# Products of the last-but-one stage placed among units 2 to 27 of the last stage, instead of among units 2 to 37

## The chip, the core and the metric

The kernel runs on one core of a Trainium2 chip. The metric is the device time of one execution in microseconds, the median of a few runs. Times of single instructions come from one profiled execution, counted from its first instruction.

## What is computed

```python
# x (1024, 24, 1024) f32, W1 (1024, 24), b1 (1024,), W2 (1024, 1024), b2 (1024,)
h = sigmoid(einsum('bts,st->bs', x, W1) + b1)
y = h @ W2.T + b2
```

The input x is about 100 MB, so nearly all of the traffic is the reading of x. The sum over t is elementwise work on x with a weight for each (s, t); the product h @ W2.T is a matrix product of 1024 x 1024 x 1024.

## The kernel before

**Tiling.** The work is cut into five stages (`STAGES`, line 19). A stage is a block of 512 rows of the batch (j, four tiles of 128) and two to four chunks of 128 columns s. The first two stages do the first 512 rows; stages 2, 3 and 4 do the other 512 rows with 3, 3 and 2 chunks. Stage 4 is the last.

**Units.** Within a stage the 24 values of t are split. The first few (six in the last stage) go to GpSimd: it multiplies their tiles by the weights and adds them up in the batch-major layout (tile `nat`, lines 485 and 495). The rest go through the PE array: a *unit* is one t and one chunk. TensorE turns its four 128x128 tiles by transposes into one PSUM bank (line 232, `xbank`), and VectorE multiplies the bank by the weight and adds it to `acc` (line 354). One more unit for each chunk turns GpSimd's sum (line 352 on VectorE). The last stage has 38 units: 0 to 31 are sixteen values of t with two chunks each, 32 and 33 turn GpSimd's sum, and 34 to 37 are the last two values of t. A unit may be turned once the bank that it takes is free, that is once the unit six before it has been added (line 221).

**Loads.** SP issues all loads of x in one order. A ring load (tile `ring`, five slots, line 201) brings one t for all chunks of the stage, so in the last stage 512 KB for two units. It waits until the last unit that read its slot, five loads before, is turned (line 200): the load of units 36 and 37 waits for unit 25. A `nat` load (line 195, 256 KB in the last stage) stands ahead of some ring loads in the queue and waits for GpSimd's sums.

**Products.** When a stage's `acc` is complete, ScalarE takes the sigmoid to `h` (line 431), and `h` and W2 are each split into a high and a low part. Each of eight outputs (128 rows x 512 columns, in one of two banks `pbank`) is summed from three products for each chunk: `h_hi` with `w_hi`, `h_hi` with `w_lo`, `h_lo` with `w_hi` (line 301, 128x512). They are issued during the *next* stage, between its units, in an order written out by `steps_due(i, v)`: after unit v of stage i, the products of stage i - 1 are issued up to step `steps_due(i, v)`. For the last stage there are 8 x 9 = 72 products; `REST` = 12 of them come behind the last unit (lines 318 to 320). VectorE adds an output to `y` (line 371) after a unit that `outs_due`, the same count divided by nine, names; so its additions of outputs stand in a fixed place between additions of units. Outputs 0 and 1 are summed with their low products behind both outputs' high ones, so output 0 is complete with product 15. An output from the third on waits on TensorE for the addition of the one two before, which had its bank (line 284).

**The end.** ScalarE's sigmoids of the last stage wait at line 450 until all eight outputs of the stage before are summed, and at line 452 for the units' additions, chunk by chunk. The last stage's own products come behind (line 332, 48 of them), then the additions and the stores.

The functions that set the order and those that follow it are these.

Of the kernel before, what the change touches and what calls it, by code (L numbers as in the profile page):

```python
# [27 lines left out]
def rec_kernel(nc, x, W1, b1, W2, b2, out):  # L28
# [12 lines left out]
    REST = 12  # L41
# [9 lines left out]
    units = []  # L51
# [38 lines left out]
    with ExitStack() as ctx:  # L90
# [64 lines left out]
        def steps_of(i):  # L155

            return 3 * chunks[i] + (fate[i] == "keep")


        def steps_due(i, v):  # L160

            steps = OUTS * steps_of(i - 1)
            if i == LAST:
                lead = chunks[i]
                return max(0, -(-(v - lead + 1) * (steps - REST) // (len(units[i]) - lead)))
            lead = 2 * chunks[i]
            span = len(units[i]) * 4 // 5 - lead
            return max(0, min(steps, -(-(v - lead + 1) * steps // span)))

        def outs_due(i, v):  # L170

            return steps_due(i, v) // steps_of(i - 1)
# [43 lines left out]
        def _(pe):  # L216
# [90 lines left out]
            for i in range(NS):  # L307
                for v in range(len(units[i])):
                    turn_unit(i, v)
                    if i == 0 and v in SETS:  # L310
                        turn_set(SETS[v])
                    if i == 0 and v in W2S:
                        turn_w2(W2S[v])
                    if i > 0:
                        for k in range(steps_due(i, v - 1) if v else 0, steps_due(i, v)):
                            product_step(i - 1, k)
# [213 lines left out]
```

## Time and profile before

| | us |
|---|---|
| median of 3 runs | 315.55 (315.52 to 315.67) |
| the profiled execution | 316.05 |
| its span, first to last instruction | 314.3 |
| TensorE busy | 262.0 (83%) |
| VectorE busy | 247.3 (79%) |
| GpSimd busy | 214.9 (68%) |
| ScalarE busy | 50.9 (16%) |
| mean granted TensorE clock | 0.973 |

The busy shares are averages over five stages and an end, which have different limits. The slices of the page show where the transfers stop, the chain of waits which engine holds the end, and timelines of one engine what stands between two instructions.

### The profile page before, as it was taken

Reading aid. Unit: us, or ns where it says so; the run is one execution under the profiler, and the core shown is the slowest. Engines: PE = TensorE matmul, PEld = TensorE weight load, DVE = VectorE, ACT = ScalarE, POOL = GpSimd, SP = SyncE. Lnnn points to the kernel's source line nnn. Section 1 sums busy time; section 2 is a strip of 40 time slices with the busy share of each in tenths; the row PEclk is TensorE's granted clock in tenths of the full one; section 3 lists DMA queues with packets and bytes.
Section 4 is the critical chain, followed back from the end, with each engine's and each line's share of the span. In section 5 each row is a group of like instructions: output and inputs, shape, how many; then the busy total and the mean of one; then the engine's idle time right before and its main releaser. Section 6 shows DMA issues by size and latency. Waiting matters only on the chain.

```text
span 314.3 us, 4779 instructions
## 1 busy us (share of the span) xinstructions
PE 262.0 (83%) x1761; PEld 223.9 (71%) x1761; DVE 247.3 (79%) x368; ACT 50.9 (16%) x85; POOL 214.9 (68%) x125
## 2 busy tenths in 40 slices
PE   0957768658889999999799999858999977989994
PEld 0946758558767888888678888746888876667773
DVE  0639998729998988889977888868887897788665
ACT  4111213202262100100600000040111113000020
POOL 3128766635469999994999977479988749994000
PEclk9989999969999999999799999979999999999999
DMA  7999999999999999999999999999999999996007
GB/s 214 392 389 387 386 387 387 401 388 386 387 387 385 386 387 387 387 385 381 373 373 373 385 384 382 376 384 373 374 373 374 368 351 339 344 348 202 2 0 268
DMA packets 67675, 109.48 MB, mean 348 GB/s; under 512 B 3642, under 2 KB 40514, under 8 KB 67652
## 3 DMA queue, kind: packets, MB, share of 16 engines
q1 hardware_dynamic: 67056, 107.06, 95.7%
q10 hardware_dynamic: 596, 2.11, 1.7%
q8 instruction: 14, 0.23, 0.3%
q14 instruction: 9, 0.07, 0.1%
HBM read 104.97 MB, written 4.19 MB: 347 GB/s over the span
## 4 chain that ended last, share of the span: by engine, by line
PE 50%; DMA 32%; DVE 5%; issue 5%; SPq 4%; ACT 2%; DVEq 0%; ACTq 0%
DMA ring<-in_r_x 32%; PE xbank L232 25%; PE pbank L301 20%; DVE acc L354 3%; PE xbank L332 3%; SPq L195 3%; SPq L201 2%; PE pbank L291 1%; ACT h L431 1%; DVE w_lo L361 1%; PE pbank L332 1%; ACT h_hi L456 1%; PE pbank L261 0%; ACT L431 0%; DVE acc L352 0%
## 5 line engine op out<-in xcount | busy, mean ns | idle before, releaser
L354 DVE SCALAR_TENSOR_TENSOR acc<-xbank,w,acc 128x512 f32<-128x512 f32 x280 | 200.4, 746 | 40.6 <-PE xbank L232 35.1
L232 PE MATMUL xbank<-ident,ring 128*128 128x128 f32 x1184 | 176.1, 284 | 44.3 <-DMA ring<-in_r_x 34.7
L232 PEld LDWEIGHTS xbank<-ident,ring 128*128 128x128 f32 x1184 | 146.5, 147 | 76.7 <-issue 30.7
L485 POOL TENSOR_TENSOR nat<-nat,w1all 128x768 f32<-128x768 f32 (+2 forms) x56 | 106.9, 1910 | 60.6 <-DMA nat<-in_r_x 47.8
L495 POOL TENSOR_TENSOR nat<-nat 128x768 f32<-128x768 f32 (+2 forms) x46 | 87.6, 1905 | 3.6
L301 PE MATMUL pbank<-w_lo,h_hi 128*128 128x512 f32 x112 | 48.8, 435 | 0.0
L301 PE MATMUL pbank<-w_hi,h_hi 128*128 128x512 f32 x112 | 48.5, 433 | 0.0
L301 PE MATMUL pbank<-w_hi,h_lo 128*128 128x512 f32 x112 | 41.0, 431 | 0.0
L431 ACT ACTIVATE h<-acc,b1col 128x512 f32<-128x512 f32 (+1 forms) x22 | 12.5, 600 | 99.7 <-DVE acc L354 64.0
L348 DVE TENSOR_SCALAR acc<-xbank,w 128x512 f32<-128x512 f32 x16 | 11.9, 748 | 13.8 <-PE xbank L232 11.6
L443 ACT COPY y<-pbank 128x512 f32<-128x512 f32 x16 | 9.4, 587 | 79.3 <-PE pbank L301 79.3
L301 PEld LDWEIGHTS pbank<-w_hi,h_hi 128*128 128x128 f32 x112 | 21.4, 191 | 0.5
L301 PEld LDWEIGHTS pbank<-w_lo,h_hi 128*128 128x128 f32 x112 | 21.4, 191 | 0.4
L500 POOL TENSOR_TENSOR h_lo<-h,h_hi 128x512 fp32r<-128x512 f32 x14 | 17.7, 1280 | 2.9 <-ACT h_hi L456 2.9
L301 PEld LDWEIGHTS pbank<-w_hi,h_lo 128*128 128x128 f32 x112 | 18.6, 191 | 0.5
L413 ACT CAST w_hi<-pbank 128x512 fp32r<-128x512 f32 x16 | 9.4, 586 | 40.6 <-PE pbank L261 40.6
L371 DVE TENSOR_TENSOR y<-pbank,y 128x512 f32<-128x512 f32 x18 | 12.2, 683 | 4.0 <-PE pbank L301 4.0
L261 PE MATMUL pbank<-ident,y 128*128 128x128 f32 x64 | 10.3, 285 | 1.4 <-DVE w_lo L361 1.4
L361 DVE TENSOR_TENSOR w_lo<-pbank,w_hi 128x512 fp32r<-128x512 f32 x16 | 10.9, 678 | 0.0
L352 DVE TENSOR_TENSOR acc<-xbank,acc 128x512 f32<-128x512 f32 x16 | 10.1, 680 | 0.1
L408 ACT COPY w1all<-pbank 128x512 f32<-128x512 f32 x12 | 7.0, 586 | 17.5 <-PE pbank L250 17.5
L261 PEld LDWEIGHTS pbank<-ident,y 128*128 128x128 f32 x64 | 7.7, 147 | 2.4 <-DVE w_lo L361 2.4
(37 smaller groups left out, 93.2 us busy)
## 6 DMA issues: line engine op xcount, KB each, us to landing
ring<-in_r_x SPq DMA_DIRECT2D x38, 1024.0 KB, 13.3
ring<-in_r_x SPq DMA_DIRECT2D x36, 768.0 KB, 11.1
nat<-in_r_x SPq DMA_DIRECT2D x20, 512.0 KB, 13.2
nat<-in_r_x SPq DMA_DIRECT2D x24, 384.0 KB, 11.5
ring<-in_r_x SPq DMA_DIRECT2D x18, 512.0 KB, 8.1
y<-in_L_rec_W SPq DMA_DIRECT2D x2, 2048.0 KB, 15.1
nat<-in_r_x SPq DMA_DIRECT2D x12, 256.0 KB, 8.7
out_y<-y ACTq DMA_DIRECT2D x4, 512.0 KB, 7.1
```

The lines of the kernel that those rows point to most:

```text
L232: mm = pe.transpose(xbank[u % XBANKS][:, j * P:(j + 1) * P], tile, ident[:, :])
L261: mm = pe.transpose(pbank[m % 2][:, j * P:(j + 1) * P], y[:, j, c * P:(c + 1) * P], ident[:, :])
L301: mm = pe.matmul(pbank[n % 2][:, :], a[:, c, rows], w[:, STAGES[i][1] + c, cols], start=r == 0, stop=r == per - 1)
L332: mm = pe.matmul(bank[:, :], a[:, c, j * P:(j + 1) * P], w[:, STAGES[LAST][1] + c, cols], start=c == 0 and k == 0, stop=c == chunks[LAST] ...
L348: nc.vector.tensor_scalar(total, bank, weight, None, ALU.mult).then_inc(unit_added, 1)
L354: nc.vector.scalar_tensor_tensor(out=total, in0=bank, scalar=weight, in1=total, op0=ALU.mult, op1=ALU.add).then_inc(unit_added, 1)
L361: nc.vector.tensor_tensor(w_lo[:, c, cols], pbank[m % 2][:, :], w_hi[:, c, cols].bitcast(F32), ALU.subtract).then_inc(w_lo_ready, 1)
L371: nc.vector.tensor_tensor(y[:, j, cols], bank[:, :], y[:, j, cols], ALU.add).then_inc(y_added, 1)
L431: nc.scalar.activation(h[:, c, rows], acc[:, c, rows], ACT.Sigmoid, bias=b1col[:, bass.ds(STAGES[i][1] + c, 1)]).then_inc(h_ready, 1)
L485: nc.gpsimd.tensor_tensor(slot, slot, row, ALU.mult).then_inc(nat_weighed, 1)
L495: nc.gpsimd.tensor_tensor(slot, slot, nat[:, (m - 2) % NATS, :, :n * P], ALU.add).then_inc(nat_added, 1)
L500: nc.gpsimd.tensor_tensor(h_lo[:, c, :], h[:, c, :], h_hi[:, c, :].bitcast(F32), ALU.subtract).then_inc(h_lo_ready, 1)
```

## The change

`steps_due` for the last stage divided the 60 products ahead of `REST` over all units behind the first two (`len(units[i]) - lead`, that is 36). It now divides them over 28 - 2 = 26 units, and a `min` keeps the count at 60 from unit 27 on.

```diff
             if i == LAST:
                 lead = chunks[i]
-                return max(0, -(-(v - lead + 1) * (steps - REST) // (len(units[i]) - lead)))
+                return max(0, min(steps - REST, -(-(v - lead + 1) * (steps - REST) // (28 - lead))))
```

The count is read in three places: TensorE's loop (line 315), VectorE's additions of outputs inside the stage (line 380) and the additions left over behind it (line 391). The order of instructions on ScalarE, GpSimd and SP does not change, nor does anything in stages 0 to 3.

TensorE, the last units of the stage. Before, units 33 to 37 (the first row is unit 33, which turns GpSimd's sum; `xbank` and `pbank` carry their numbers) and the first products behind them:

```order
L232 MATMUL xbank1<-ident,nat 128x128 x4
L301 MATMUL pbank1<-w_hi,h_lo 128x512 x2
L232 MATMUL xbank2<-ident,ring 128x128 x4
L301 MATMUL pbank0<-w_hi,h_hi 128x512
L232 MATMUL xbank3<-ident,ring 128x128 x4
L301 MATMUL pbank0<-w_lo,h_hi 128x512
L301 MATMUL pbank0<-w_hi,h_hi 128x512
L232 MATMUL xbank4<-ident,ring 128x128 x4
L301 MATMUL pbank0<-w_lo,h_hi 128x512
L301 MATMUL pbank0<-w_hi,h_hi 128x512
L232 MATMUL xbank5<-ident,ring 128x128 x4
L301 MATMUL pbank0<-w_lo,h_hi 128x512
```

Now, from unit 27 (the first row) to unit 37 and the products behind it:

```order
L232 MATMUL xbank1<-ident,ring 128x128 x4
L301 MATMUL pbank0<-w_hi,h_hi 128x512
L301 MATMUL pbank0<-w_lo,h_hi 128x512
L232 MATMUL xbank2<-ident,ring 128x128 x4
...
L232 MATMUL xbank0<-ident,nat 128x128 x4
L232 MATMUL xbank1<-ident,nat 128x128 x4
...
L232 MATMUL xbank5<-ident,ring 128x128 x4
L301 MATMUL pbank0<-w_hi,h_lo 128x512 x3
```

The products that stood between units 28 and 37 are gone from there; units 28 to 37 follow each other, and behind unit 37 come the twelve of `REST`, as before.

VectorE, the front of the last stage, now, from the additions of units 5 and 6 to that of output 1 (behind unit 10):

```order
L354 SCALAR_TENSOR_TENSOR acc<-xbank3,w1,acc 128x512
L354 SCALAR_TENSOR_TENSOR acc<-xbank4,w1,acc 128x512
L371 TENSOR_TENSOR y<-pbank0,y 128x512
L354 SCALAR_TENSOR_TENSOR acc<-xbank5,w1,acc 128x512
L354 SCALAR_TENSOR_TENSOR acc<-xbank0,w1,acc 128x512
L354 SCALAR_TENSOR_TENSOR acc<-xbank1,w1,acc 128x512
L354 SCALAR_TENSOR_TENSOR acc<-xbank2,w1,acc 128x512
L371 TENSOR_TENSOR y<-pbank1,y 128x512
```

Before, the addition of output 0 stood behind that of unit 7, one later, and that of output 1 behind unit 13. All six additions of outputs inside the stage have moved forward; the last one was ahead of the last three units and is now ahead of the last twelve.

## Rows read from the trace of the kernel before

**Rows 1.** The page: busy shares, then slices of the span.

```profile
PE 262.0 (83%) x1761; PEld 223.9 (71%) x1761; DVE 247.3 (79%) x368; ACT 50.9 (16%) x85; POOL 214.9 (68%) x125
...
DMA  7999999999999999999999999999999999996007
```

**Rows 2.** The chain that ended last, from 276.92: start us, us, what.

```profile
276.92 7.88 DMA ring<-in_r_x
284.80 0.14 issue
284.94 0.63 PE xbank L232 x4
285.56 0.47 PE pbank L301 x2
286.03 0.44 PE xbank L232 x4
...
294.38 0.44 PE xbank L232 x4
294.82 2.99 PE pbank L301 x13
297.80 0.03 ACTq L452
...
297.88 0.41 ACT h L431
```

**Rows 3.** Waits from 297 us on: us in total, times, longest.

```profile
ACT h L431 <- PE pbank L301: 35.8, 1, 35.8
```

**Rows 4.** Ring loads, line 201: the last (issued 284.2), then all from 250.

```profile
L201 SPq DMA_DIRECT2D ring<-in_r_x x1: 368/368/368, 284.2 to 284.2; - x1
...
DMA to landing us min/median/max: 6.1/6.1/6.1
...
DMA to landing us min/median/max: 6.1/8.0/9.5
```

**Rows 5.** Timeline of TensorE: units 4, 6, 12, 18, 24, 25, 26, 28, 36, 37.

```profile
262.61 0.63 PE L232 MATMUL xbank<-ident,ring 128*128 128x128 f32 x4 [0.98 <-DMA ring<-in_r_x]
...
264.82 0.63 PE L232 MATMUL xbank<-ident,ring 128*128 128x128 f32 x4 [0.45 <-DVE acc L354]
...
270.72 0.63 PE L232 MATMUL xbank<-ident,ring 128*128 128x128 f32 x4 [0.46 <-DMA ring<-in_r_x]
...
276.71 0.63 PE L232 MATMUL xbank<-ident,ring 128*128 128x128 f32 x4 [0.50 <-DVE acc L354]
...
282.67 0.63 PE L232 MATMUL xbank<-ident,ring 128*128 128x128 f32 x4 [0.48 <-DMA ring<-in_r_x]
...
283.60 0.60 PE L232 MATMUL xbank<-ident,ring 128*128 128x128 f32 x4
...
284.94 0.63 PE L232 MATMUL xbank<-ident,ring 128*128 128x128 f32 x4 [0.50 <-DMA ring<-in_r_x]
...
286.78 0.60 PE L232 MATMUL xbank<-ident,ring 128*128 128x128 f32 x4
...
293.31 0.60 PE L232 MATMUL xbank<-ident,ring 128*128 128x128 f32 x4
...
294.22 0.60 PE L232 MATMUL xbank<-ident,ring 128*128 128x128 f32 x4
```

**Rows 6.** Timeline of VectorE at the front of the stage.

```profile
269.39 0.69 DVE L371 TENSOR_TENSOR y<-pbank,y 128x512 f32<-128x512 f32 x1 [2.25 <-PE pbank L301]
270.00 4.03 DVE L354 SCALAR_TENSOR_TENSOR acc<-xbank,w,acc 128x512 f32<-128x512 f32 x6
```

**Rows 7.** Timeline of GpSimd: its last sum.

```profile
285.60 1.29 POOL L495 TENSOR_TENSOR nat<-nat 128x512 f32<-128x512 f32 x1
```

**Rows 8.** TensorE's transposes, 262.6 to 286.8, by line: busy, mean, idle before.

```profile
L232 PE MATMUL xbank<-ident,ring 128*128 128x128 f32 x97 | 14.9, 275 | 3.8 <-DMA ring<-in_r_x 2.4 <-DVE acc L354 0.9
```

**Rows 9.** A stage boundary: timeline; stretches (us, PE busy, clock, DMA, GB/s).

```profile
209.11 4.13 PE L232 MATMUL xbank<-ident,ring 128*128 128x128 f32 x24 [3.77 <-DMA ring<-in_r_x]
...
208.40:211.80 3.40, 2.69 (x13) 0.50 1.06 373
```

## The prediction

> **What bounds the kernel now.** I read four views in this order. The page [rows 1] gives the span, the busy shares and the forty slices: the DMA row is full for 36 slices, 6 in the 37th and 0 after it until the output is stored, while the core goes on for some 27 us. So the kernel is bound by its transfers for nine tenths of its time and by something else at the end, and a change in the last stage must be read from that end. The chain of waits [rows 2] tells what that is. It follows the load issued at 276.92 to its landing at 284.80, and from there to 297.80 it is TensorE alone, without a gap: units (four transposes, 0.44 us) and products (0.23 us each) in turn, then 13 products in 2.99 us. Only then does ScalarE start the sigmoids of the last stage, because line 450 makes it wait until all eight outputs of the stage before are summed; the waits [rows 3] show the same from ScalarE's side. The stretch behind 297.80 (16.5 us of the span: sigmoids, splits, 48 tail products, additions, stores) is in the same order in both kernels.
>
> The third view, the load queue [rows 4], says how far TensorE lags behind its data: the last ring load (units 36 and 37) is issued at 284.2 and lands 6.1 us later, at 290.3. TensorE's timeline [rows 5] has unit 36 at 293.31. So the last data lie ready for 3.0 us. The fourth is the same timeline before that: from unit 4 (262.61) to unit 28 (286.78) it shows idle pieces in front of units 4, 12, 24 and 26, that end with a landing, and in front of 6 and 18, that VectorE ends.
>
> **What the change moves.** Nothing is added or removed. Of the 72 products of the stage before, 12 stay behind the last unit as before; the other 60 were spread over 36 units, 1.67 each, and are now spread over 26 units, 2.31 each, and are done with unit 27. By the formula, 44 were issued by unit 27 before and 60 are now: 16 products change sides, 16 x 0.23 = 3.7 us of TensorE's time. VectorE's six additions of outputs (line 371) follow the same count and move forward; the two others stay behind the splits. SP's and GpSimd's programs are unchanged in order.
>
> **Behind unit 27.** Before, units 28 to 37 and 16 products took from 286.78 to 294.82 or so, 10 x 0.44 + 16 x 0.23 = 8.1 us. Now they are 10 x 0.44 = 4.4 us, if nothing else holds them.
>
> **Ahead of unit 28.** Units 4 to 27 carried 40 products and now carry 55. Before: 24 x 0.44 + 40 x 0.23 = 19.8 us of work in 24.2 us, so about 4.4 us idle. The new work is 24 x 0.44 + 55 x 0.23 = 23.2 us. It fits with 0.9 us to spare, provided the idle time can take it. I think it can, since a product needs no new data: TensorE used to come early to a load, and now comes as it lands. The fit shows in rates too: a unit with 2.31 products is 0.97 us, and the loads that TensorE waited for landed at 262.5, 270.6 (270.72 less 0.14), 282.5 and 284.8, over units 4 to 26 one unit in 22.3 / 22 = 1.01 us. Unit 26 cannot start before 284.94 in either kernel. After it come 0.63 + 0.44 + 4 x 0.23 = 2.0 us, so unit 28 starts at 286.9, against 286.78. The added products cost nothing up to here because waiting for loads covers them; without that cover they would cost the whole 3.5 us.
>
> **The last units.** Eight units from 286.9 at 0.44 end at 290.4, and the last load lands at 290.3, 0.14 more until the first transpose [rows 2], so 290.5. Both limits meet within a tenth. Unit 36, released from a wait, takes 0.63; from unit 37's start to the end of the products it took 294.22 to 297.80 = 3.58 with 13 products, now 12, so 3.35. End: 290.5 + 0.63 + 3.35 = 294.5, against 297.80: **3.3 us** less. That is also the most the change can give while the last load lands when it did.
>
> **What is late next.** First, the ring load: it waits until unit 25 is turned. Unit 24 still waits for its load (282.67), and behind it stand three products where there were two, plus what TensorE lags; I put unit 25 about 0.4 us later (from 283.60 to 284.0). The load behind it then is issued 0.4 us later. Bounds for the landing: not later at all, if its 6.1 us are queueing, or the full 0.4. For queueing speaks that the loads issued before it took a median of 8.0 us [rows 4] with the DMA row full, and that the last one, with fewer behind it, took the least. I take 0.2, the middle. The Trainium skill ("DMA: Bandwidth & Descriptors", the section on the anatomy of one DMA) puts the fixed part of a transfer at about 2 us, by which most of the 6.1 us would be queue and the sum would be 3.3 instead of 3.1; no run here has a ring load on an empty queue.
>
> Second, VectorE. An addition of a unit takes 0.66 us in a row (six in 4.03, the last 0.74) [rows 6], a bare unit 0.44, so VectorE is now the slower of the two behind unit 27. It can be up to six units behind, since there are six banks. Unit 37 is turned only after unit 31's addition; from there units 32 to 36, which the first sigmoid needs, are five additions, 3.3 us, against 0.6 + 12 x 0.23 = 3.4 us for TensorE's rest. So VectorE at its worst comes out level, and unit 37's addition is wanted only 1.2 us later, behind four sigmoids. It costs between 0 and 0.2; I take 0. At the front of the stage VectorE stood still for 2.25 us at 269.39, waiting for output 0 at product 15 [rows 6]; now unit 8 instead of unit 10 holds that product, so that stop gets no longer.
>
> Third, GpSimd: the sums of unit 32 are ready at 285.60 + 1.29 = 286.9 [rows 7], and TensorE now asks at 288.7. Free by 1.8 us.
>
> **Sum.** -3.3 + 0.2 = **-3.1 us**. The profiled execution: span 314.3 to 311.2, its time 316.05 to 312.95. The profiled one lies 0.5 us over the median of 315.55; taking the same off the median gives **312.4 us**.
>
> **Rivals.**
> 1. TensorE keeps part of its idle time (0.12). Four of its waits in the stretch are for loads, others for VectorE's banks [rows 8]; products cannot fill a wait that stands in the wrong place, as the order is fixed. If 2.2 us of idle stay (half of 4.4) where 0.9 fit, unit 28 comes at 262.61 + 23.2 + 2.2 = 288.0, 1.1 us later, and the gain shrinks to 2.0: 313.5.
> 2. Nothing is won (0.05). If all 4.4 us of idle stay, unit 28 comes at 290.2 and the end at 297.8 again, since the products only changed places: 315.5. What speaks against it is that of the 3.8 us that the trace calls idle, loads end 2.4 [rows 8], and a load lands by its queue and not by TensorE's pace.
> 3. The clock (0.03). Behind unit 27 TensorE does bare units, and may stand still for the last load. In the trace TensorE sat idle 3.77 us up to 209.11, and in the 3.4 us that followed the granted clock was 0.50, the 1.2 GHz level: 24 transposes took 4.13 us instead of 24 x 0.11 = 2.6, so 1.5 us lost [rows 9]. Once here: a gain of 1.6, 313.9. Through the other waits of the last stage, of 1 us and less, it stayed at 1.00. The Trainium skill ("TensorE: Matmul & The Clock Gate", the section on the clock gate) says that the low level is the default and activity releases it; that speaks against leaving the last units bare. By that rule, with the trace agreeing only for the long gap, this would be the outcome if the last load came late.
> 4. Slower (0.06), through the ring. The place is line 200: each ring load waits for the unit ten before. If TensorE falls behind by L at unit 25 and the load then takes the median 8.0 us rather than 6.1, it lands at 284.2 + L + 8.0, and the end is 4.1 us behind that (0.14 + 0.63 + 3.35). From L = 1.5 on this passes 297.8; with L = 2.4 it is 0.9 later: 316.4. Against it speaks that the bare 6.1 was taken by the very load in question.
>
> **Chances and range.** The forecast has 0.74. A measurement tells 0.2%, 0.6 us, from no change. Faster by more than that are the forecast and rivals 1 and 3: 0.89. Within it rival 2: 0.05. Slower rival 4: 0.06. The range goes from 311.8 (the last load landing 0.4 earlier and nothing late) to 313.9 (rivals 1 and 3).
>
> **What would show it.** The chain after should have the products' end near 294.5 to 294.8 (before 297.80) and a ring load's landing directly ahead of unit 36, near 290.4. Unit 28 near 286.9 shows that idle time covered the products; near 288 or later shows rival 1. Idle time of TensorE between 262.6 and 286.9 should fall from 4.4 us to about 1. A granted clock under 1.00 behind 288 would be rival 3; a last load issued behind 285.5 and landing behind 293 rival 4. The 16.5 us behind the products should stay within 0.1. The forecast is wrong in its base if unit 26 starts much behind 284.94, since then the stretch ahead was not paced by loads.

## The result, and the profile after

| | before | after |
|---|---|---|
| median, us | 315.55 (5 runs, 315.38 to 315.76) | 311.89 (5 runs, 311.74 to 312.71) |
| ratio, 95% interval | | 0.9891 (0.9879 to 0.9903) |
| span of the profiled execution | 314.3 | 310.1 |
| first transposes of the last stage (unit 0) | 258.10 | 257.69 |
| unit 28 starts | 286.78 | 286.18 |
| end of the last product of the stage before | 297.80 | 293.64 |
| from there to the end of the span | 16.5 | 16.5 |

The kernel is faster by 3.66 us, 1.1%. In the profiled execution after, unit 0 of the last stage starts 0.41 us earlier, although the stages ahead of it are the same in both kernels; this is the scatter between executions. So of the 4.2 us between the spans, 0.4 are scatter and 3.75 are what this execution won in the last stage. A second profiled execution of the changed kernel (experiment 9) won 3.4 by the same count, so single tenths of this account are scatter too. Below, "on the clock of before" means with 0.41 us added.

The page after, as [rows 1]:

```profile
PE 257.8 (83%) x1761; PEld 220.0 (71%) x1761; DVE 246.4 (79%) x368; ACT 50.9 (16%) x85; POOL 215.2 (69%) x125
...
DMA  7999999999999999999999999999999999999007
```

Busy shares say nothing of what happened: TensorE and VectorE are at 83% and 79% as before. The slices say little more. The 37th, which was at 6, is full, but a slice is a fortieth of the span, so it now covers 279.1 to 286.8 and covered 282.9 to 290.7 before. What counts is the end behind the last landing: 24.0 us before (290.3 to 314.3) and 20.5 after (289.6 to 310.1).

The chain that ended last, as [rows 2] (start us, us, what):

```profile
284.38 0.59 PE xbank L232 x4
284.97 0.47 PE pbank L301 x2
285.43 0.44 PE xbank L232 x4
285.87 0.47 PE pbank L301 x2
286.34 4.54 PE xbank L232 x40
290.88 2.76 PE pbank L301 x12
293.71 0.41 ACT h L431
294.14 0.24 DVE h_hi L387
294.41 0.30 DVE h_lo L389
294.85 4.35 PE xbank L332 x18
```

Ten bare units are one piece of 4.54 us: no wait stands among them, not even for the last load. (A timeline gives the start of an instruction, the chain the end of the one before it. So unit 28 starts at 286.18 in the table and at 286.34 here.) The chain holds no load either. Ahead of the piece lie units and products in turn, back to 261.70, where the first products waited for `h_hi`. TensorE's transposes up to unit 28, as [rows 8], with their idle time behind the bar:

```profile
L232 PE MATMUL xbank<-ident,ring 128*128 128x128 f32 x101 | 15.2, 273 | 0.1
```

3.8 us of idle time have become 0.1. The last ring load, as [rows 4]:

```profile
L201 SPq DMA_DIRECT2D ring<-in_r_x x1: 368/368/368, 283.9 to 283.9; - x1
...
DMA to landing us min/median/max: 5.7/5.7/5.7
```

VectorE at both ends of the stage, as [rows 6] (the stop for output 0, then all that follows the addition of unit 27):

```profile
267.17 0.69 DVE L371 TENSOR_TENSOR y<-pbank,y 128x512 f32<-128x512 f32 x1 [1.29 <-PE pbank L301]
...
286.81 2.73 DVE L354 SCALAR_TENSOR_TENSOR acc<-xbank,w,acc 128x512 f32<-128x512 f32 x4 [0.15 <-PE xbank L232]
289.46 1.28 DVE L352 TENSOR_TENSOR acc<-xbank,acc 128x512 f32<-128x512 f32 x2
290.65 2.72 DVE L354 SCALAR_TENSOR_TENSOR acc<-xbank,w,acc 128x512 f32<-128x512 f32 x4
294.14 0.23 DVE L387 CAST h_hi<-h 128x128 fp32r<-128x128 f32 x1 [0.77 <-ACT h L431]
```

From 286.81 to 293.37 VectorE adds ten units without a pause, and its last addition ends only 0.27 us ahead of TensorE's last product (293.64). It then stands still for 0.77 us, until the sigmoid behind that product is done. So TensorE still holds the end, but VectorE has come close behind it.

### The profile page after: what moved, and what is told of

Its sections match the earlier page's. It is cut to its first block, busy times and chain, and to the rows that moved or that the text cites. A ratio compares the mean times of both kernels' runs of the same rounds, so it can differ in the third digit from the quotient of the medians.

```text
span 310.1 us, 4779 instructions
## 1 busy us (share of the span) xinstructions
PE 257.8 (83%) x1761; PEld 220.0 (71%) x1761; DVE 246.4 (79%) x368; ACT 50.9 (16%) x85; POOL 215.2 (69%) x125
## 4 chain that ended last, share of the span: by engine, by line
PE 51%; DMA 31%; DVE 7%; issue 5%; ACT 3%; SPq 1%; DVEq 0%; ACTq 0%
DMA ring<-in_r_x 31%; PE xbank L232 25%; PE pbank L301 20%; DVE acc L354 4%; PE xbank L332 3%; ACT h L431 2%; DVE w_lo L361 2%; ACT h_hi L456 1%; PE pbank L291 1%; PE pbank L332 1%; PE pbank L261 0%; DVE acc L352 0%; ACT L431 0%; SPq L195 0%; SPq L201 0%
## 5 line engine op out<-in xcount | busy, mean ns | idle before, releaser
L232 PE MATMUL xbank<-ident,ring 128*128 128x128 f32 x1184 | 171.5, 279 | 44.2 <-DMA ring<-in_r_x 36.0
L232 PEld LDWEIGHTS xbank<-ident,ring 128*128 128x128 f32 x1184 | 142.2, 144 | 75.7 <-issue 27.9
L250 PE MATMUL pbank<-ident,w 128*128 128x128 f32 x48 | 7.7, 286 | 1.5 <-DVE w_lo L361 1.5
```

What stands on the lines that cost most here:

```text
L232: mm = pe.transpose(xbank[u % XBANKS][:, j * P:(j + 1) * P], tile, ident[:, :])
```

## The experiments

The times are medians; "before" in each comparison is the kernel before on the same chip. Each edit is made to the changed kernel, except where said.

**1. Spread over units 2 to 32.**

```diff
-... // (28 - lead))))
+... // (33 - lead))))
```

> The 60 products ahead of the twelve are spread over units 2 to 32 instead of 2 to 27. By the formula 52 are then issued by unit 27, so 8 of the 16 moved products are back behind it, 8 x 0.23 = 1.8 us. Theory A (idle time in front of landed loads took up the moved products): by unit 27 TensorE has 52 x 0.23 us of products and still waits for loads, so nearly the whole 1.8 us comes back at the end: 313.5 to 313.8, about half of the gain. Rival B (the gain is VectorE's, whose stop for output 0 went from 2.25 to 1.29 us): output 0 is now asked for behind unit 7 as before the change, so most of the gain goes: 315.0 to 315.5. Rival C (the gain is the earlier start of the bare units, any number of them does): 312 as with 28.

Measured: 313.69 (313.60 to 313.74), ratio 0.994 (0.9924 to 0.9957). That is Theory A's number. TensorE's transposes, 262.6 to 286.8:

```profile
L232 PE MATMUL xbank<-ident,ring 128*128 128x128 f32 x98 | 15.0, 275 | 1.3 <-DMA ring<-in_r_x 1.3
```

Idle time in front of landed loads is back, by 1.3 us, and about half of the gain has gone. Rival C (any number of bare units) is out. VectorE's stop for output 0 is as short here as in the changed kernel:

```profile
267.94 0.69 DVE L371 TENSOR_TENSOR y<-pbank,y 128x512 f32<-128x512 f32 x1 [1.29 <-PE pbank L301]
```

So the loss against the changed kernel does not come from that stop. Nor did the shorter stop bring loads sooner: SP issued the load that unit 26 waits for at 276.92 before and at 276.51 after, which is 276.92 on the clock of before. Rival B is out.

**2. Six products behind the last unit instead of twelve.**

```diff
-    REST = 12
+    REST = 6
```

> REST is 6 instead of 12: 66 products in units 2 to 27, six behind the last unit. Theory L (the end is the last load's landing, two bare units and the products behind them): six products fewer behind it, 6 x 0.23 = 1.4 us less than the changed kernel, 310.5. Theory F (TensorE has no idle time left between unit 4 and the last product, so only its total work counts and their order does not): 0, so 311.9, with the bare units starting 1.4 us later and no wait for the last load.

Measured: 312.72 (311.52 to 313.45, four runs), ratio 0.9907 (0.9878 to 0.9936), and in a second round on another chip (experiment 12) 312.21 (311.74 to 313.51, six runs), ratio 0.9904. Neither theory: not 1.4 us less, and not steady at the same. The profiled execution (313.45) shows two things. First its chain:

```profile
285.85 0.45 PE xbank L232 x4
...
286.33 0.03 DVE acc L354
...
286.99 0.27 DVE y L371
...
287.59 0.80 DVE acc L354 x2
...
293.39 0.74 DVE acc L354
...
294.14 0.14 DVE h_hi L387
...
294.74 5.97 PE xbank L332 x18
```

From 286.33 on it is VectorE, not TensorE. The last of TensorE's products:

```profile
291.64 0.86 PE L301 MATMUL pbank<-w_hi,h_lo 128*128 128x512 f32 x3
294.74 0.47 PE L332 MATMUL xbank<-w_hi,h_hi 128*128 128x512 f32 x1 [2.24 <-DVE h_lo L389]
```

They end at 292.50, counted from unit 0's start (257.45 here, 257.69 in the changed kernel) 0.9 us sooner than with 12. So Theory L had most of TensorE's side right, and F had it wrong: small pieces of waiting were left that the idle column does not show. The timelines give their size. From unit 0's start to unit 28's, TensorE took 28.49 us in the changed kernel and 29.14 with REST 6, with six products (1.38 us) more, so 0.73 less for the rest: the changed kernel has five units of 0.50 to 0.63 us in its chain there, REST 6 one of 0.53, all others 0.44. The ten bare units took 4.45 and 4.28 us, which gives the other 0.17. But an addition of an output more stands ahead of unit 28's, unit 28 comes later, and VectorE's first split starts 36.60 us after unit 0 where it was 36.45. The gain on TensorE is given back by VectorE.

Second, 18 tail products take 5.97 us where they took 4.35. Stretches of TensorE in that execution (us, PE busy, clock, DMA, GB/s):

```profile
292.30:295.80 3.50, 1.26 (x6) 0.99 0.00 0
295.80:299.20 3.40, 3.40 (x10) 0.50 0.00 0
299.20:302.60 3.40, 3.40 (x16) 1.00 0.00 0
```

TensorE was idle for 2.24 us, started the tail at the full clock, and 1 us later (294.74 to 295.80) fell to the 1.2 GHz level and ran there for 3.4 us. That costs 5.97 - 4.35 = 1.6 us.

**3. Eighteen products behind the last unit.**

```diff
-    REST = 12
+    REST = 18
```

> REST is 18 instead of 12: 54 products in units 2 to 27, eighteen behind the last unit. Theories L and F agree here: the loads hold units 24 and 26 where they are, TensorE waits in front of them again (idle time 1 to 1.5 us in the stretch up to unit 28), and six more products stand behind the last unit, 6 x 0.23 = 1.4 us more than the changed kernel: 313.3. A rival (order of products is indifferent altogether): 311.9.

Measured: 313.24 (313.04 to 313.40), ratio 0.9927 (0.9912 to 0.9942), as expected. TensorE's transposes again, 262.6 to 286.8:

```profile
L232 PE MATMUL xbank<-ident,ring 128*128 128x128 f32 x100 | 15.0, 274 | 1.1 <-DMA ring<-in_r_x 1.1
```

Six products taken out from ahead of unit 28 turn into 1.1 us of waiting for loads, and are paid behind the last unit. Experiment 1 spreads the same products wider, this one takes some out of the stretch; both give idle time back, and the time with it.

**4. Spread over units 2 to 21.**

```diff
-... // (28 - lead))))
+... // (22 - lead))))
```

> The 60 products are spread over units 2 to 21, three behind each unit, 1.13 us for each unit where the loads bring one in about 1.0. Theory F: TensorE is not idle, falls behind the loads by some 1 to 1.5 us around unit 22, and catches up in sixteen bare units; 311.9 unless it has to wait for the last load. The rival from the ring (the load of units 36 and 37 waits for unit 25, which comes later, and the load takes its 6 us whatever the time of its issue): unit 25 is turned no later than before since no product stands behind unit 22, so at most 0.3 later: 311.9 to 312.3.

Measured: 312.64 (312.08 to 313.41), ratio 0.991 (0.9892 to 0.9928): 0.7 us over the changed kernel's 311.89, more than either line allowed. The chain:

```profile
283.04 1.76 PE xbank L232 x16
284.80 0.02 issue
284.82 6.36 DMA ring<-in_r_x
291.18 0.14 issue
291.31 1.06 PE xbank L232 x8
292.37 2.77 PE pbank L301 x12
```

My expectation had unit 25 no later, as no product stands behind unit 22. But TensorE was behind by then: units 22 to 25 follow at 0.44 us each from 283.04, so unit 25 is turned at 284.80, and with it the last load goes out 0.9 us later than in the changed kernel (283.9). It lands 6.36 us later, and two units and twelve products stand behind that. In this execution the products end at 295.14, 1.5 us after the changed kernel's; 0.3 of that is its later start of the stage.

The late issue of that one load does not explain its landing. Counted from unit 0's start it went out at 26.9 us, and with REST 6 it went out at 26.7 to 26.9 in four profiled executions and landed at 31.5 to 32.1; here it landed at 33.2. What differs is the queue ahead of it. TensorE is late for the units before as well, so SP waits for free ring slots longer (13.7 us between 258 and 290, against 9.0 in the changed kernel and 10.4 with REST 6), and the DMA engines run short of work. A stretch of this kernel, then the same of the changed one (us, PE busy, clock, DMA, GB/s):

```profile
284.00:286.00 2.00, 2.00 (x21) 1.00 0.70 224
```

```profile
284.00:286.00 2.00, 2.00 (x14) 1.00 0.97 315
```

This is the forecast's rival 4, in part: too much density ahead holds back the loads, not the last one alone. Of the four spreads tried (22, 28, 33 and 38 units), 28 lies between two losses.

**5. The wait for the outputs moved from the sigmoid to the first split.**

```diff
+                    if c == 0 and j == 0:
+                        dve.wait_ge(out_summed, OUTS * LAST)
                     dve.wait_ge(h_ready, first_h[LAST] + c * JT + j + 1)
...
-                    act.wait_ge(out_summed, OUTS * i)
+                    if i < LAST:
+                        act.wait_ge(out_summed, OUTS * i)
```

> With the change, plus: ScalarE's sigmoids of the last stage no longer wait for the eight outputs of the stage before; VectorE waits for them in front of the first split, which is what overwrites the operands of those products. The profile of the changed kernel has the last product ending at 293.64, the sigmoid at 293.71 to 294.12, the first split at 294.14. If the wait for the outputs is what holds the sigmoid, the split starts at 293.7 instead, 0.4 us less: 311.5. If unit 36's addition by VectorE held it (it ends about 292.7 to 293.4), nothing: 311.9.

Measured: 311.36 (310.85 to 311.55), ratio 0.9873 (0.9857 to 0.9889). The first split follows the last product at once:

```profile
291.05 2.76 PE pbank L301 x12
293.81 0.02 issue
293.84 0.24 DVE h_hi L389
```

The sigmoid is off the chain. Against the kernel before on the same chip (315.25) this is 3.9 us less, where the changed kernel has 3.7 and, in experiment 9, 3.5. So 0.2 to 0.4 of the expected 0.4 show, and the intervals of the two ratios overlap.

**6. The first chunk's splits in a free slot.** The products of the stage before read slots 0 to 2 of `h_hi` and `h_lo`; the first chunk's splits now go to slot 3, and only the second chunk's wait for the outputs.

```diff
+    SLOT = (3, 1)
...
+                    if c == 1 and j == 0:
+                        dve.wait_ge(out_summed, OUTS * LAST)
...
-                    nc.vector.tensor_copy(h_hi[:, c, rows], h[:, c, rows]).then_inc(tail_hi, 1)
+                    nc.vector.tensor_copy(h_hi[:, SLOT[c], rows], h[:, c, rows]).then_inc(tail_hi, 1)
...
-                    act.wait_ge(out_summed, OUTS * i)
+                    if i < LAST:
+                        act.wait_ge(out_summed, OUTS * i)
```

> With the change, plus: the splits of the last stage's first chunk go to slot 3 of h_hi and h_lo, which the products of the stage before do not read, so that sigmoid and splits of that chunk wait for VectorE's additions alone; the second chunk's splits wait for the outputs. If TensorE's last products are what the end waits for, the first split moves from 294.14 to behind VectorE's last addition (it ends at 293.37 in the changed kernel's trace), about 0.8 us less: 311.1. VectorE would then hold the end, and not TensorE. If the order of engines is not what I think, 311.5 (as with the moved wait) or 311.9.

Measured: 310.95 (310.70 to 311.06), ratio 0.9861 (0.9844 to 0.9877). From 288.82 on its chain goes through VectorE alone to the first split:

```profile
292.65 0.74 DVE acc L355
293.39 0.14 DVE h_hi L390
...
294.00 4.37 PE xbank L333 x18
```

**7. The same tail with the order of products of before.** The line of `steps_due` is that of the kernel before, the rest is experiment 6.

> The order of products of the kernel before (60 products over all units), with only the first chunk's splits in slot 3 and the sigmoids free of the wait for the outputs. If TensorE's stream of units and products holds the end in the kernel before, its products still end where they did (297.8 in the trace of before), but the tail products follow without the wait for sigmoid and split, which was 299.01 - 297.80 = 1.2 us: 314.4. If VectorE held it, nothing: 315.5. Against the changed kernel with the same tail (310.95) it tells what the order of products is worth when the wait behind it is gone: 3.4 us.

Measured: 313.91 (313.59 to 314.01), ratio 0.9955 (0.9938 to 0.9972). 1.3 us against the kernel before: the wait of 1.2 us between product and tail product is gone, because TensorE goes from one to the other:

```profile
294.21 2.97 PE pbank L302 x13
297.19 4.08 PE xbank L333 x18
```

So in the kernel before TensorE's stream held the end. With a free tail the order of products is worth 313.91 - 310.85 = 3.1 us (310.85 is experiment 10, on the same chip), where 3.4 was expected.

**8. Six products behind the last unit, with the tail of 6.**

> REST 6 with the tail of the run before it. With REST 6 alone the times lay between 311.5 and 313.5, and the profiled one had TensorE idle for 2.24 us ahead of the tail products and the granted clock at 0.50 for 3.4 us right behind, 1.6 us lost. If VectorE's additions hold the end (they ran without a gap from 286.3 to 294.05), its first split comes where it came, at 294.05 less nothing, TensorE is idle as long, and the clock can fall as before: 311.4 to 313.4, scattered. If the outputs' wait held it, 310.6 and steady.

Measured: 313.38 (312.03 to 313.83, four runs), ratio 0.9933 (0.9909 to 0.9957). The profiled one (312.03) has the same 2.24 us of idle time and the clock at 1.00 behind it. Its first split follows VectorE's last addition at once:

```profile
293.70 0.74 DVE acc L355
294.44 0.14 DVE h_hi L390
```

That the wait for the outputs held REST 6 is out; VectorE held it.

**9 and 10. The changed kernel and the one of experiment 6 again, side by side.**

> The changed kernel again, on the chip and beside the runs of the one that follows: 311.9, with the last products' end at 293.6 and TensorE without idle time ahead of unit 28.

> The changed kernel with the free tail again: 310.95, 0.9 us under the changed kernel, the first split right behind VectorE's last addition.

Measured: 311.79 (311.59 to 312.11), ratio 0.9891 (0.9876 to 0.9905), and 310.85 (310.68 to 311.04), ratio 0.986 (0.9845 to 0.9875). The version with the free tail is faster than both kernels, by 4.4 us than before and by 0.9 us than after; its slowest run lies below the fastest of the changed kernel. The profile of experiment 9 repeats that of the result: 0.2 us of idle time in front of the transposes from 262.6 to 286.8, ten bare units in one piece, and the last product's end at 293.59.

```profile
286.26 4.56 PE xbank L232 x40
290.82 2.77 PE pbank L301 x12
```

Counted from unit 0's start (257.31), the last product ends at 236.28 us here, at 235.95 in the first profiled execution and at 239.70 in the kernel before.

**11 and 12. REST 6 with the idle time filled, and without.** Eight products that nobody reads fill most of TensorE's idle time ahead of the tail.

```diff
+            pe.wait_ge(unit_added, UNITS - XBANKS + 1)
+            for k in range(8):
+                pe.matmul(xbank[UNITS % XBANKS][:, :], w_hi[:, 0, 0:P], w_hi[:, 1, 0:BANK], start=True, stop=True)
             for c in range(chunks[LAST]):
```

> REST 6 with eight extra products of W2 with itself into a free bank, behind the last real product, whose result is overwritten; they fill 8 x 0.23 = 1.8 of the 2.24 us in which TensorE was idle there, and nothing waits for them longer than it waits for VectorE anyway. If it is the idle time that lets the clock fall, the times are steady and near those of REST 6 at full clock, 311.4 to 311.7, and the stretch behind the idle time has clock 1.00. If the clock falls for another reason, the times stay scattered up to 313.4. If the extra products are in the way, 0.2 to 0.5 more.

> REST 6 again beside it: scattered from 311.4 to 313.4 in steps of the clock's fall, median above the one with the extra products by 0.5 to 1.6.

Measured: 311.85 (311.42 to 312.45, four runs) with the filling, 312.21 (311.74 to 313.51, six runs) without. The two intervals of the ratios (0.9873 to 0.9903, 0.9887 to 0.9922) overlap, and the medians lie 0.4 us apart, less than the 0.5 to 1.6 expected. In the filled kernel the idle time ahead of the tail is 0.42 us. Two stretches of TensorE around the start of the tail, first of the filled kernel, then of the unfilled one. The first stretch is busy in the one and a third busy in the other; the clock stays up in both, so behind the same idle time that came with a fall in experiment 2 it did not fall here:

```profile
292.30:295.70 3.40, 2.98 (x14) 1.00 0.00 0
...
295.70:299.10 3.40, 3.40 (x17) 1.00 0.00 0
```

```profile
292.30:295.70 3.40, 1.16 (x5) 1.00 0.00 0
...
295.70:299.10 3.40, 3.40 (x16) 1.00 0.00 0
```

So with 2.24 us of idle time the clock fell in one of three profiled executions. Of the fourteen runs with REST 6 and no filling (experiments 2, 8 and 12), six lie above 313.3, where one fall of 1.6 us would put them; of the four filled ones, none. That fits with the idle time as the cause. It isn't shown, for two reasons: four filled runs are few (at a share of six in fourteen, four in a row without a fall come about one time in ten, an estimate from these counts), and the clock in that stretch is known for the profiled executions alone.

## Why the prediction was right, point by point

**Direction and mechanism: right.** It forecast 312.4 (311.8 to 313.9) with 3.1 us off; it is 311.89, with 3.66 off, near the low end of the range. The mechanism came as described; that the time is half a microsecond better than forecast comes from two small terms and from scatter. The steps:

- *The idle time ahead of unit 28 takes up the 15 added products.* Right, and more fully than said. The prediction wanted idle time down from 4.4 to about 1; the trace has 0.1 of its own count of 3.8 (0.2 in experiment 9). Experiments 1 and 3 give the idle time back in part and the time with it.
- *Unit 28 at 286.9.* It started at 286.18, on the clock of before 286.6, 0.3 early. In experiment 9 it started 28.79 us after unit 0 (286.10), which is 286.9 on the clock of before. So this term is right within the scatter. Its last part, 2.0 us behind unit 26, was read too long: the rows have 286.78 - 284.94 = 1.84 for the same two units and four products [rows 5], and they took 1.84 again.
- *The last load 0.2 us later.* This is a term that was mis-sized. The load was issued 0.1 us later than before and landed 0.3 sooner in the first profiled execution; in experiment 9 it was issued 0.4 later, as forecast, and landed 0.1 later. The bound "no later" was the better one, and the sum's bounds left out "sooner", which only the range allowed. All other profiled executions but that of experiment 4 agree: the load was issued between 26.0 and 26.9 us after unit 0's start and landed between 31.5 and 32.5, the late issues no later than the early ones. At least 1.3 of the prediction's 6.1 us are no fixed cost, since with REST 6 the same load took 4.8 (experiments 8 and 12). The Trainium skill ("DMA: Bandwidth & Descriptors", the section "Anatomy of one DMA — SWDGE (gpsimd) path") gives its fixed 2 us for transfers that GpSimd issues, and adds the time to move the bytes; by its formula 512 KB take 3.2 us, an estimate, so that about half of the 6.1 would be queue, not most. SP issues these loads, and no run here has one on an empty queue.
- *Unit 36 released from a wait: 0.14 + 0.63.* It was not, and this is the other mis-sized term. The load landed just as TensorE came (ten bare units in 4.54 us, 4.56 in experiment 9), so there was no 0.14 and the unit took 0.45, as all ten did. This is 0.3 us, in both executions. So the sentence that 3.3 us is the most that the change can give, as long as the last load lands when it did, was too low: experiment 9 won 3.4 with a landing 0.1 later.
- *VectorE comes out level.* Right: its last addition ended 0.27 us ahead of the last product, and it waited 0.77 us for the first sigmoid. The prediction priced it at nothing, which holds for this kernel. It did not say that the next step would run into it, as experiment 2 did.
- *GpSimd free by 1.8 us, the 16.5 us behind the products unchanged.* Both right: GpSimd's last sum ended at 286.54, TensorE turned it at 288.03, and 310.1 - 293.64 = 16.5.

**The rivals.** Rival 1 (idle time stays in part) is out here, and is what experiments 1 and 3 made by hand. Rival 2 (nothing won) is out. Rival 3 (the clock) did not come with the change, where TensorE's longest idle piece behind 288 is the 1.22 us ahead of the tail and the granted clock stays at 1.00; with REST 6 it came in one of three profiled executions. Rival 4 (the ring) did not come with 28 and came in part with 22.

**What stays open.** That the clock accounts for the scatter of REST 6 is likely but not shown, and why it fell in one execution and not in two others behind the same idle time is not known. Nor is it shown why the last load's landing varies by 1 us between executions.

## What to carry to other kernels

When the end of a kernel is one engine's stream and that engine waited for loads a little earlier, move deferrable work ahead into the waits, and size it so that the engine comes just as the load lands. Too little leaves idle time (experiments 1, 3), too much delays the release of the buffers that the loads need, until the DMA engines run short of work (experiment 4). Look at once for the second engine: with 3.7 us won, VectorE was done only 0.3 us ahead of TensorE, and the next 0.9 us came from a buffer slot that let it go on, not from a better order.

## What the runs showed of the hardware

- The granted clock fell to the 1.2 GHz level after 2.24 us of idle TensorE, once in three profiled executions, and only 1 us after work had begun again; it stayed there for 3.4 us and cost 1.6 us. After 3.77 us of idle time in the kernel before [rows 9] it had fallen too. After 1.22 us ahead of the tail it did not in the changed kernel's two profiled executions. The Trainium skill ("TensorE: Matmul & The Clock Gate", the section "Why this matters for your kernels") advises against longer idle gaps between bursts of matmuls. The fall after 3.77 us agrees with it; the fall of experiment 2 came behind a shorter gap than the page warns of, and the two executions without one show that such a gap does not always bring it.
- A ring load of 512 KB, the last of its stage, took between 4.8 and 6.4 us in the fourteen profiled executions. While the queue ahead of it was full, it did not go by the time of its issue: issued 26.0 to 26.9 us after unit 0's start, it landed at 31.5 to 32.5 in thirteen of them (issued at 26.2 it landed at 31.9, at 26.7 in experiment 12 at 31.5, at 26.9 in experiment 11 at 32.0). In the fourteenth (experiment 4) the DMA share of the two microseconds up to 286 was 0.70 where the changed kernel has 0.97, and it landed at 33.2.
- A unit of four transposes took 0.44 us in a stream and 0.63 us where TensorE had waited for it; pieces between the two (0.50 to 0.59) stand in the changed kernel's chain where the idle column shows 0.1 us in all.
